# Adapter rows for the transposes on VectorE requested through GpSimd's DMA queue instead of ScalarE's, with two low-part steps drawn forward

## The reference, cut to what matters

```python
x = x + _L0_cond_ref(x, L0_cond_weight, L0_cond_scale_log, condB_codebook, L0_cond_lora_A, L0_cond_lora_B)
def lora_add(base, inp, A, B):
    Ab = A[layer_idx][lora_indices]
    Bb = B[layer_idx][lora_indices]
    t = jnp.einsum('bri,bni->bnr', Ab, inp)
    return base + jnp.einsum('bor,bnr->bno', Bb, t) * SCALE
gate = lora_add(jnp.einsum('bnh,fh->bnf', x, W_gate), x, A_gate, B_gate)
up = lora_add(jnp.einsum('bnh,fh->bnf', x, W_up), x, A_up, B_up)
act = jax.nn.silu(gate) * up
down = lora_add(jnp.einsum('bnf,hf->bnh', act, W_down), act, A_down, B_down)
x = x + down
```

## Time and profile before

| | |
|---|---|
| median of 3 runs | 1605.49 us (1604.38 to 1606.32) |
| profiled execution, its own time | 1605.84 us |
| span in the profile | 1604.2 us |
| matmuls | 6968, TensorE busy 98% of the span |
| VectorE, ScalarE, GpSimd busy | 77%, 35%, 34% |
| granted TensorE clock, mean | 0.994 |
| A_down and B rows for stage 1 | 264 DMAs, all through ScalarE's queue |

### The profile page before, as it was taken

How to read it: one execution, slowest core, us unless ns; L and a number is a source line. 1 busy time by engine, 2 the same in 40 slices (tenths; PEclk the granted TensorE clock), 3 DMA queues, 4 the chain that set the end, 5 groups by cost and what they waited for, 6 DMA issues and landing times.

```text
span 1604.2 us, 21109 instructions
## 1 busy us (share of the span) xinstructions
PE 1573.2 (98%) x6968; PEld 1294.7 (81%) x6968; DVE 1240.1 (77%) x1575; ACT 566.3 (35%) x1006; POOL 538.7 (34%) x401
## 2 busy tenths in 40 slices
PE   7999998999999999998999999999999999999999
PEld 5888886788888888886888888888888888888887
DVE  7998968788878999999867787887676576785443
ACT  6411135433333333354433333333343233233231
POOL 4410013465654555644344555555310000000000
PEclk9999999999999999999999999999999999999999
DMA  9552173677878888883335666654277677686463
GB/s 291 132 112 79 48 234 91 178 202 223 229 205 196 229 231 224 237 296 93 105 120 133 181 175 177 186 175 150 81 217 212 159 179 193 153 223 206 151 188 119
DMA packets 368460, 281.25 MB, mean 175 GB/s; under 512 B 225120, under 2 KB 266848, under 8 KB 368224
## 3 DMA queue, kind: packets, MB, share of 16 engines
q1 hardware_dynamic: 246976, 240.77, 51.6%
q10 hardware_dynamic: 119296, 33.33, 8.9%
q0 software_dynamic: 2080, 5.80, 1.8%
HBM read 166.27 MB, written 110.85 MB: 173 GB/s over the span
## 4 chain that ended last, share of the span: by engine, by line
PE 79%; DVE 1%; issue 1%; DVEq 0%
PE bank L1827 21%; PE bankA L1827 14%; PE bankC L1827 14%; PE bank L2063 10%; PE bankC L2063 7%; PE bankA L2063 6%; PE bankT L2063 3%; PE bankT L1878 1%; PE bankT L1879 1%; PE bankC L1843 1%; PE bank L1843 1%; PE bankA L1843 1%; DVE opl L1491 0%; DVE ev L1438 0%; DVE opl L1497 0%
## 5 line engine op out<-in xcount | busy, mean ns | idle before, releaser
L985 ACT CAST rh<-wt 128x512 fp32r<-128x512 f32 x253 | 155.0, 620 | 371.3 <-PE bank L1827 76.6
L1328 DVE TENSOR_TENSOR rl<-wt,rh 128x512 fp32r<-128x512 f32 x253 | 237.0, 944 | 40.2 <-ACT rh L985 40.1
L1497 DVE TENSOR_TENSOR opl<-opl,oph 128x512 fp32r<-128x512 f32 (+1 forms) x154 | 107.7, 701 | 155.6 <-ACT oph L1122 155.3
L1827 PE MATMUL bank<-xh,rh 128*128 128x512 f32 x528 | 205.7, 390 | 2.2 <-issue 2.2
L1827 PE MATMUL bank<-xl,rh 128*128 128x512 f32 x528 | 205.6, 389 | 0.0
L1827 PE MATMUL bank<-xh,rl 128*128 128x512 f32 x528 | 205.5, 389 | 0.0
L1122 ACT CAST oph<-opl 128x512 fp32r<-128x512 f32 (+1 forms) x154 | 95.5, 621 | 268.9 <-DMA opl<-LT_d 260.8
L1827 PE MATMUL bankC<-xh,rh 128*128 128x512 f32 x352 | 139.3, 396 | 7.1 <-DVE xl L1337 3.9
L1827 PE MATMUL bankC<-xl,rh 128*128 128x512 f32 x352 | 138.9, 395 | 0.0
L1827 PE MATMUL bankC<-xh,rl 128*128 128x512 f32 x352 | 138.8, 394 | 0.0
L1827 PE MATMUL bankA<-xh,rl 128*128 128x512 f32 x352 | 137.7, 391 | 0.0
(11 more groups left out here) (209 smaller groups left out, 3670.0 us busy)
## 6 DMA issues: line engine op xcount, KB each, us to landing
opl<-LT_d SPq DMA_DIRECT2D x148, 256.0 KB, 2.9
WT_d<-wt SPq DMA_DIRECT2D x88, 256.0 KB, 3.1
RT_d<-dt SPq DMA_DIRECT2D x70, 256.0 KB, 3.3
opl<-RT_d SPq DMA_DIRECT2D x70, 256.0 KB, 3.8
LT_d<-ev ACTq DMA_DIRECT2D x60, 256.0 KB, 2.6
wb<-WT_d SPq DMA_DIRECT2D x44, 256.0 KB, 3.5
wt<-WT_d SPq DMA_DIRECT2D x44, 256.0 KB, 3.5
dn<-in_L_cond_W_down_dram SPq DMA_DIRECT2D x86, 128.0 KB, 3.9
```

The source lines that it names most:

```text
L985: nc.scalar.copy(rh[:, v % RING, 0:KH * rows], wsrc(mm, RSRC[p])).then_inc(s_hi, 1)
L1328: dv.tensor_tensor(rl[:, v % RING, 0:KH * rows], wsrc(mm, RSRC[p]), rh[:, v % RING, 0:KH * rows].bitcast(f32), ALU.subtract).then_inc(s_lo, 1)
L1497: dv.tensor_tensor(opl[0:rows, L_AT[n % NL], :], opl[0:rows, L_AT[n % NL], :].bitcast(f32), oph[0:rows, L_AT[n % NL], :].bitcast(f32), ALU ...
L1827: last = te.matmul(OUT[p], a[:, u % RING, cols], b[:, OPND[p], k, :], start=k == 0 and n == 0, stop=k == KH - 1 and n == 2 and (p in (0, 1 ...
```

## The change

`load_bn` and `load_an` are moved, unchanged but for the engine, into GpSimd's program, and are issued at other places: both for iteration 0 behind the gathers, once group 23 of stage 0's `main` is done (their tiles lie over a weight buffer of stage 0); `load_bn(1)` at step 1; `load_bn(it + 2)` at `(m, p) == (1, 4)` behind `w_s3`; `load_an(it)` at `(m, p) == (0, 1)`, behind the first two `act_sum` and ahead of `w_s12`. ScalarE issues none of them any more.

Two further edits belong to it. In the first block of each half GpSimd's `w_s12(mm + 1)` waits until all seven x operands have their low parts. And VectorE makes `lo` and the last `x_lo` of step 3 in step 2, ahead of `take(mm, 2)`.

```diff
@@ gpsimd
+                def load_bn(it):
+                    h, j = it // NJ, jof(it)
+                    rows = rows_of(j)
+                    wait(gp, s_bt, 2 * it)
+                    for t in range(2):
+                        for g, src in enumerate((Bg_d, Bu_d)):
+                            q = 2 * t + g
+                            gp.dma_start(bn[q * Q:(q + 1) * Q, 0:2 * rows // Q, :],
...
+                def load_an(it):
+                    h, j = it // NJ, jof(it)
+                    wait(gp, s_ar, it)
+                    for half in range(2):
+                        for i in range(NI):
+                            i_ = min(i, rows_of(j) // Q - 1)
+                            gp.dma_start(an[i * Q:(i + 1) * Q, half, :, :],
...
+                gp.wait_ge(s_gat1, 3 * NB * 16)
+                gp.wait_ge(s_main, TURN[KD - 3, NC - 1] + 1)
+                load_bn(0)
+                load_an(0)
                 w_s12(0)
                 w_s3(0)
...
                     if p == 2 and 0 <= mm + 1 < NM:
+                        if mm in (0, NH):
+                            gp.wait_ge(s_xlo, 14 + mm // NH * 14)
                         w_s12(mm + 1)
...
                     if p == 4 and 0 <= mm + 1 < NM:
                         w_s3(mm + 1)
+                    if (u == 1 or (m, p) == (1, 4)) and it + 1 + m < NIT:
+                        load_bn(it + 1 + m)
+                    if (m, p) == (0, 1) and 0 < it < NIT:
+                        load_an(it)
@@ scalar
-                act.wait_ge(s_gat1, 3 * NB * 16)
-                load_bn(0)
...
-                load_bn(1)
-                load_an(0)
...
-                    if (m, p) == (1, 6) and it != NJ - 1 and it + 2 < NIT:
-                        load_bn(it + 2)
-                    if (m, p) == (1, 6) and it != NJ - 1 and it + 1 < NIT:
-                        load_an(it + 1)
-                    if (it, m, p) == (NJ, 0, 5):
-                        load_bn(NJ + 1)
-                        load_an(NJ)
@@ vector
-                    if RING <= u + RING - 2 < 7 * NM:
+                    if RING <= u + RING - 2 < 7 * NM and u % END not in (3, 3 + END // 2):
                         lo(u + RING - 2)
...
-                    if u <= 3:
+                    if u <= 2:
                         x_lo(0, u + 3)
-                    if 7 * (NM // 2) - 3 <= u < 7 * (NM // 2) + 4:
+                    if 7 * (NM // 2) - 3 <= u < 7 * (NM // 2) + 3:
                         x_lo(1, u - 7 * (NM // 2) + 3)
+                    if u in (2, 2 + END // 2):
+                        lo(u + RING - 1)
+                        x_lo(it // NJ, 6)
```

More of the change, by code:

```diff
@@ L904, in dn_sums @@
                         tt(b21, b21, b22, ALU.subtract).then_inc(s_ds, 1)
+                def load_bn(it):
[6 more added lines that the diff above has]
+                            gp.dma_start(bn[q * Q:(q + 1) * Q, 0:2 * rows // Q, :],
+                                         src.rearrange("f b r -> f (b r)")[f_at(0, j):f_at(0, j) + 2 * rows, (2 * h + t) * CR:(2 * h + t + 1) * CR]
+                                         .rearrange("(a c) r -> c a r", c=Q)).then_inc(s_bn, 16)
+                def load_an(it):
[5 more added lines that the diff above has]
+                            gp.dma_start(an[i * Q:(i + 1) * Q, half, :, :],
+                                         Ad_d[2 * h * CR:2 * (h + 1) * CR, f_at(half, j) + i_ * Q:f_at(half, j) + (i_ + 1) * Q]
+                                         .rearrange("(t c) r -> c t r", t=2)).then_inc(s_an, 16)
                 gp.dma_start(idx[:, :], adapter.rearrange("(o b) -> o b", o=1)).then_inc(s_idx, 16)
@@ L1015, in load_wa @@
                                       .rearrange("(f c) d -> c f d", c=Q)).then_inc(s_wa, 16)
[L1017 to L1036, removed]
                 def b_hi(n):
```

## The result

Before, 1605.68 us in the median of 18 runs; after, 1600.58 us in the median of 18 (1596.99 to 1604.27). The ratio is 0.9967, with a 95% interval from 0.9958 to 0.9975: 5.1 us less, where 12.7 were forecast. The profiled execution took 1599.27 us, 6.6 less than that of before (1605.84); its span is 1597.6.

The account below looks back on a forecast made before the run. TensorE, busy 98% of the span, was taken as the bound, so only lost time could return. Gains of 3.7 + 5.0 + 4.0 = 12.7 us from 1605.84 gave 1593.1, stated as 1593, range 1585 to 1602.

Parts of the forecast that it names:

- the three stretches: 246 to 266, 302 to 313 and 715 to 747 us, where TensorE lost 7.3, 5.8 and 9.9 us, together 23.0.
- First stretch: 246 to 266 us: waits for x's low parts go, 3.6 of 7.3 us lost stay; gain 3.7 (2 to 7.3).
- The wait for `ts`: First stretch: TensorE waits 1.9 us for this adapter operand, plus 1.7 us at half pace behind it.
- Second stretch: 302 to 313 us: the 3.60 us wait for `al` shrinks to about 0.8; gain 5.0 (1 to 5.8).
- Third stretch: 715 to 747 us: GpSimd's held sums no longer slow x's low part; gain 4.0 of 9.9 (1 to 6).
- GpSimd's issues: 264 DMA issues move to GpSimd, some 7.0 us an iteration; hidden by its room and cover, cost 0.
- 0.3 off: Third stretch: deduction because delayed activation sums fall beside `ts_lo` and `ride_lora` may wait longer.
- here the DMA issues matter little: Third stretch: the gain was put down to GpSimd's new wait on `s_xlo`, not to moving the DMAs.
- Cover 8.2 us, use 3.0: Full iteration: the sum behind `an` comes 3.0 us later; VectorE's queue covers 2.6, the ring 5.6; cost 0.
- dear issues: Rival: `an` issues ahead of `w_s12` cost from 1.2 us each and stall full iterations; 1646 us at 1.61; slower, chance 0.10.
- The partial gain: Rival: VectorE bounds the three stretches and returns only its gaps, 2 + 2 + 1 = 5 us; 1600.5, chance 0.16.
- Rows that arrive: `bn` is asked for six steps ahead of its transpose, `an` nine, 16 and 24 us; cost 0.

Follow-up runs that it names:

- e3: The changed kernel without GpSimd's wait on `s_xlo` in the second half (the one in the first half stays); 1601.57 us, ratio 0.9971.
- e6: The changed kernel with GpSimd's eight issues of `an` two steps earlier, where GpSimd waits for a store; 1597.84 us, ratio 0.9944.
- e7: The changed kernel with the edits of e5 and e6 together; 1594.10 us, ratio 0.9922.
- e5: The changed kernel with GpSimd's activation sums at the change of halves held until both `ts_lo` pairs are done, `w_s3` ahead of them; 1597.69 us.
- e2: The changed kernel without VectorE's new order and GpSimd's waits on `s_xlo`, only the DMAs moved; 1599.12 us, ratio 0.9958.
- e11: The kernel before with new order and `s_xlo` waits, activation sums held behind `ts_lo` and `w_s3`, ScalarE still issuing the DMAs; 1605.32 us.
- e12: e7 with only the first `ride_lora` of each half one product later, `late_lora` as it was; 1592.64 us, ratio 0.9919.

## Why the prediction was wrong in size

*The bound, the method and the direction* held: the three stretches are where the time was, and two of the three gave 9.1 us back where 8.7 were forecast for them.

*First stretch, 3.7 us.* Right: 5.3 in the profiled execution, 3.6 to 3.9 in e3 to e6. The wait for `ts` was put at 1.9 us and measured 2.09. Behind it the clock stayed up in the profiled execution (262.37 to 262.59), which the forecast hadn't allowed; in e3 to e6 it fell, as forecast. Holds and new order alone bring 0.2 here, the DMA move alone 4.1.

*Second stretch, 5.0 us.* 6.0 us came back up to product 21, 2.2 went again up to 28. What the forecast missed is that only the wait for `al` was followed. TensorE, 6 us further on, then caught up with VectorE at the next operand, `ad`:

```profile
324.14 0.35 DVE L1458 TENSOR_TENSOR ad<-tm,ad 128x64 fp32r<-128x64 f32 x2
```

TensorE starts at 324.55, 0.06 us behind the end of that row. With `an` early this loss is 0.2 us, but 1.3 us less come back at product 20, so that the stretch changes by 0.7 us at most (e6 against after; e7 against e5 by -0.1).

*Third stretch, 4.0 us: this step failed.* It came out at -2.0, which is 6.0 of the 6.1 us between the forecast's 12.7 and the 6.6 of the profiled execution; 1.6 of them are the loss at 157, which is GpSimd's issues, below. Its first half is right (the low parts of x at 2.36 us, 4.5 us back from 157 to 160). Wrong is that the sums "then fall beside `ts_lo`" at a price of "0.3 off": from product 160 to 164 it was 5.2 us. I had the row for the price, 2.83 us, and charged it as if one `ts_lo` more could not matter; the first was lengthened by 1.95 us, on an engine with no gap there, with `al` of the same queue behind it. With the sums moved, the loss at 162 falls from 4.6 to 0.7 us (e6 against e7), and the stretch gains 2.1 us. The new order was put at nothing in this half without a reason: e3 against e2 shows a loss of 2.8 us. Also wrong is "here the DMA issues matter little": e11 shows ScalarE's issues as the next link of that chain once the sums are out of the way, with a wait for `ts` of 1.85 us where e7 has 0.88.

*GpSimd's issues, 0 us.* The price of one was right (0.53 us for `an`, 0.58 for `bn`, against 0.51 and 0.56). The cover was not. "Cover 8.2 us, use 3.0" followed one consumer, the weight sum to its product. Behind the same block stood the activation sums, their stores on SyncE, and x in SyncE's list behind these; and VectorE's queue, in order, passes on a late cast to `al`. The profiled execution lost 1.6 us at 157, and at twice the length the full iterations lost some 25 us, where 8.2 us of cover said none. Of the mechanisms among the rivals this is that of dear issues: not with a dear issue, but with its place.

*The partial gain* (1600.5) has the measured time (1600.58) by luck. It gives 2, 2 and 1 us back in the three stretches; measured are 5.3, 3.8 and -2.0. And e7 and e12 show that VectorE wasn't the end of it: 6.5 and 8 us more were there, most of it in the order of GpSimd's list. That the time also lies within the forecast's own bounds is owed to their width: the third stretch is outside its term's 1 to 6 us.

*Rows that arrive, 0 us,* right: no wait for `bn` or `an` in the trace. Between 330 and 700 TensorE waits nowhere, as was said too.

## What to carry over

When instructions move to an engine with room, its busy share says nothing about the place: follow each thing that stands behind them in its list, and what stands behind that in the next engine's list, down to the queue that only issues transfers. Put the block where the engine already waits for something far away. And a wait that holds back work doesn't remove a collision; look at what the work will then fall beside.

## What the runs showed of the hardware

*Beside GpSimd's sums `ts_lo` waited for the rest of a sum, twice.* `ts_lo` is two operations, 0.88 us together. Beside sums of GpSimd it took 2.83: the sums ended at 725.44 (723.69 + 1.75) and 726.87 (725.51 + 1.36), and the pair ended at 727.15, 0.28 us after the second. So each operation seems to have run only when a sum had ended, in the gap before the next. In e5, with one sum beside it that ended at 726.37 (724.62 + 1.75), the pair took 1.80 us and ended at 727.05. The addition next to it, which reads one operand from PSUM, took 1.23 us beside the next sum, as everywhere (mean 1.22 of 44). The Trainium skill ("SBUF — State Buffer", the section on two separate sides) has this rule: VectorE and GpSimd share one port pair under an exclusive lock, held for a whole instruction, and a VectorE operation with two inputs in SBUF counts when the GpSimd one reads SBUF. The trace agrees, down to the addition from PSUM. The forecast used only the part of that section on DMAs, and asked whether transposes count there too. By the trace they don't: the eight issues took 4.23 or 4.24 us with VectorE's transposes beside them and without.

*The same price seems to be paid far off too.* Of the 27 us by which VectorE works longer, 12.1 are `al` (1089 ns in the mean instead of 951) and 13.6 `rl`, both with two inputs in SBUF; the additions out of PSUM stay at 1.22 us. I read them as the same collision, on the ground of that pattern alone; it isn't shown. With `an` early VectorE needs 15 us less again:

```profile
PE 1570.4 (98%) x6968; PEld 1292.5 (81%) x6968; DVE 1252.6 (78%) x1575; ACT 570.0 (36%) x1006; POOL 678.3 (42%) x665
```

*A DMA issue on ScalarE* holds it as long as one on GpSimd: eight took 3.81 us there, 4.24 here.
